# Two moves around the seam between an attention and a quantized feed-forward: where a small chain of scale arithmetic runs, and in which order the LoRA factors are written

## The reference, cut to what matters

```python
x = x + tanh(g_xattn[0]) * L0_xattn(layernorm(x), ctx, ctx)      # linear attention
x = x + tanh(g_ffn[0])   * L0_ffn(layernorm(x), ...)             # NF4 weights with LoRA, width 2752
x = x + tanh(g_xattn[1]) * L1_xattn(layernorm(x), ctx, ctx)      # autocorrelation attention by FFT
x = x + tanh(g_ffn[1])   * L1_ffn(layernorm(x), ...)             # linear layer with LoRA and column norm

def L0_ffn(x1, ...):
    Wg, Wu, Wd = (NF4[codes] * absmax per 64, transposed)        # three dequantized matrices
    y1 = x1 @ Wg + x1 @ g_lora_a @ g_lora_b
    y2 = x1 @ Wu + x1 @ u_lora_a @ u_lora_b
    x3 = relu(y1) * y2
    return x3 @ Wd + x3 @ d_lora_a @ d_lora_b
```

## Time and profile before

| what | value |
|---|---|
| median of 3 executions | 2161.8 us (2161.77 to 2164.0) |
| profiled execution | 2167.11 us, its span 2165.1 us |
| TensorE busy | 2052.2 us, 95% of the span, mean granted clock 0.977 |
| VectorE, ScalarE, GpSimd busy | 51%, 54%, 31% |
| attention | about 0 to 180.5 us |
| feed-forward | about 180.8 to 1600 us |
| tail | to 2165.1 us |

### The profile page before, as it was taken

How to read it: one execution, slowest core, us unless ns; L and a number is a source line. 1 busy time by engine, 2 the same in 40 slices (tenths; PEclk the granted TensorE clock), 3 DMA queues, 4 the chain that set the end, 5 groups by cost and what they waited for, 6 DMA issues and landing times. The chain is left out here.

```text
span 2165.1 us, 25964 instructions
## 1 busy us (share of the span) xinstructions
PE 2052.2 (95%) x9634; PEld 1023.6 (47%) x9634; DVE 1098.7 (51%) x1951; ACT 1175.9 (54%) x1851; POOL 663.7 (31%) x640
## 2 busy tenths in 40 slices
PE   7985999999999999999999999999975899999997
PEld 5772444444444444444444444444432455555543
DVE  5774252442624335253352524335257788888852
ACT  6993755656566565665656566565613334344321
POOL 3432211112121121211112121121225676667741
PEclk9997999999999999999999999999987899999999
DMA  6632211112122121221221111111130011111000
GB/s 222 201 127 61 77 49 59 48 51 70 58 65 69 55 69 54 69 69 55 64 63 55 49 55 49 55 49 51 44 125 24 12 40 49 49 49 46 13 30 29
DMA packets 64925, 136.76 MB, mean 63 GB/s; under 512 B 8992, under 2 KB 13728, under 8 KB 64800
## 3 DMA queue, kind: packets, MB, share of 16 engines
q1 hardware_dynamic: 64800, 135.11, 19.1%
HBM read 122.49 MB, written 12.58 MB: 62 GB/s over the span
## 5 line engine op out<-in xcount | busy, mean ns | idle before, releaser
L682 ACT ACTIVATE first<-first 128x512 f32<-128x512 int32 x1008 | 632.7, 628 | 28.0
L920 PE MATMUL ps_ring<-xT_hi,gu_hi 128*128 128x512 f16 x1376 | 524.2, 381 | 1.7 <-POOL gu_lo L758 1.7
L920 PE MATMUL ps_ring<-xT_lo,gu_hi 128*128 128x512 f16 x1376 | 523.7, 381 | 0.0
L920 PE MATMUL ps_ring<-xT_hi,gu_lo 128*128 128x512 f16 x1376 | 523.2, 380 | 0.0
L812 DVE SCALAR_TENSOR_TENSOR wt<-first,w_scale,absm 128x512 f32<-128x512 f32 x132 | 98.8, 749 | 478.5 <-ACT first L682 477.4
L758 POOL TENSOR_TENSOR gu_lo<-wt,gu_hi 128x512 f16<-128x512 f32 x88 | 102.6, 1166 | 765.2 <-ACT gu_hi L688 765.2
L831 DVE SCALAR_TENSOR_TENSOR X<-ps_ring,ffn_gain,X 128x512 f32<-128x512 f32 x352 | 259.8, 749 | 135.3 <-PE ps_ring L943 135.3
L943 PE MATMUL ps_ring<-dn_hi,hid_hi 128*128 128x512 f16 x704 | 266.9, 379 | 0.0
L943 PE MATMUL ps_ring<-dn_hi,hid_lo 128*128 128x512 f16 x704 | 266.7, 379 | 0.0
L943 PE MATMUL ps_ring<-dn_lo,hid_hi 128*128 128x512 f16 x672 | 254.6, 379 | 0.0
L920 PEld LDWEIGHTS ps_ring<-xT_hi,gu_hi 128*128 128x128 f16 x1376 | 135.1, 98 | 171.7 <-issue 14.5
(11 more groups left out here) (203 smaller groups left out, 2683.1 us busy)
## 6 DMA issues: line engine op xcount, KB each, us to landing
first<-in_codes SPq DMA_DIRECT2D x132, 256.0 KB, 2.8
absm<-in_absmax SPq DMA_DIRECT2D x264, 128.0 KB, 3.0
X<-in_x SPq DMA_DIRECT2D x16, 512.0 KB, 4.3
c_in<-in_ctx SPq DMA_DIRECT2D x16, 512.0 KB, 5.3
cT<-in_ctxT SPq DMA_DIRECT2D x16, 512.0 KB, 3.6
xT_hi<-in_ctx SPq DMA_DIRECT2D x8, 1024.0 KB, 7.1
out<-X SPq DMA_DIRECT2D x16, 512.0 KB, 2.6
wide<-in_w SPq DMA_DIRECT2D x8, 512.0 KB, 4.7
```

Source lines behind the costliest of these rows:

```text
L682: act.activation(level[u % 2][:], codes[u % RING] if k == 0 else level[u % 2][:], ACT.Prelu, bias=bias, scale=scale, alpha=alpha).then_inc ...
L920: mm = pe.matmul(o[:], w[c][:, m, k, :], xx[:, k, ts], start=(q == 0), stop=(q == 3 * KD - 1))
```

## The change

Two edits. First, the scales' parts now run inside middle steps. With AT = 9: SyncE issues the three bound loads before the loads of b = 4; ScalarE squares at the start of step 8; VectorE reduces in step 9, reads the maxima in step 10, the spread results in step 11 and runs the chain of tiny results in step 13, each time right after `kvm` and ahead of the offset of line 465; TensorE's three small products stand in steps 10 and 11, after the product of line 434, in an upper part of `psE`, and two waits are added ahead of the turning of `ek` in steps 11 and 12 (`left`); GpSimd's square roots stand at the start of step 12. One more small copy is made (`every[:, 9:12]` is read apart). Second, at the opening of the feed-forward the LoRA factors are written in the order of use: `lora_b` first, then m = 0 and the first unit, m = 1 and the second unit, and m = 2 and `l_gain` after all six units. TensorE waits for each m only before the first unit that uses it.

```diff
-    ps_top, ps_all = ps[0:9, 0:P], ps[:, BANK:BANK + 12]
+    ps_top, ps_all = ps[0:9, BANK:BANK + P], ps[:, BANK + 2 * P:BANK + 2 * P + 12]
+    AT = 9
-    OWN, DIAG, EVERY = 6, 8, 9
+    OWN, READ, DIAG, EVERY = 6, 8, 9, 10
     def pool_part(pool, i):
-        if i == TILES:
+        if i == AT + 3:
     def act_part(act, i):
-        if i == TILES - 2:
+        if i == AT - 1:
     def pe_part(pe, i):
-        if i == TILES:
+        if i == AT + 1:
             pe.wait_ge(step, OWN)
-            pe.matmul(ps_top, own[:, 0:9], ident[:], start=True, stop=True).then_inc(top_mm, 1)
             pe.wait_ge(const_set, 3)
             pe.matmul(ps_all[:, 9:12], ones[:], own[:, 9:12], start=True, stop=True)
+            pe.matmul(ps_top, own[:, 0:9], ident[:], start=True, stop=True).then_inc(top_mm, 1)
+        if i == AT + 2:
             pe.wait_ge(step, DIAG)
             pe.matmul(ps_all[:, 0:9], ones[0:9, :], diag[:], start=True, stop=True).then_inc(all_mm, 1)
     def dve_part(dve, i):
-        if i == TILES - 1:
+        if i == AT:
             dve.wait_ge(squared, 3)
...
-        if i == TILES:
+        if i == AT + 1:
             dve.wait_ge(top_mm, 1)
             dve.reduce_max(top[:], ps_top, AX.X).then_inc(step, 1)
-            dve.wait_ge(step, 7)
+            dve.tensor_copy(every[:, 9:12], ps_all[:, 9:12]).then_inc(step, 1)
+            dve.wait_ge(step, 8)
             dve.tensor_scalar(diag[:], ident[0:9, 0:9], top[:], None, ALU.mult).then_inc(step, 1)
+        if i == AT + 2:
             dve.wait_ge(all_mm, 1)
-            dve.tensor_copy(every[:], ps_all).then_inc(step, 1)
-        if i == TILES + 1:
+            dve.tensor_copy(every[:, 0:9], ps_all[:, 0:9]).then_inc(step, 1)
+        if i == AT + 4:
             dve.wait_ge(norms_done, 1)
...
+    def left(pe, i):
+        if i == AT + 2:
+            pe.wait_ge(step, READ)
+        if i == AT + 3:
+            pe.wait_ge(step, EVERY)
...
+                    if b == 4:
+                        scales_sp(sp)
...
-                scales_sp(sp)
```

```diff
 ScalarE, opening of the feed-forward
                 act.wait_ge(la_in, 48)
-                for m in range(3):
+                lora_parts(0)
+                for m in range(2):
                     act.activation(lora_a[:, m], la_f[m], ACT.Copy, scale=ab_scale[0:LROWS, 0:1]).then_inc(la_hi, 1)
-                lora_parts(0)
                 for u in range(AHEAD):
                     w_hi(0, u)
+                    if u == 3:
+                        act.activation(lora_a[:, 2], la_f[2], ACT.Copy, scale=ab_scale[0:LROWS, 0:1]).then_inc(la_hi, 1)
 VectorE
-                for m in range(3):
+                def lora_wide(m):
                     dve.wait_ge(la_hi, m + 1)
                     dve.scalar_tensor_tensor(lora_a[32:64, m], ...).then_inc(la_done, 1)
                 lora_parts(0)
+                lora_wide(0)
+                weights(0, 0, first=True)
+                lora_wide(1)
+                weights(0, 1, first=True)
+                for u in range(2, AHEAD):
+                    weights(0, u)
+                lora_wide(2)
                 dve.wait_ge(mag_in, 16)
                 dve.tensor_scalar(l_gain[:], ...).then_inc(gain_done, 1)
-                for u in range(AHEAD):
-                    weights(0, u, first=u < 2)
 TensorE
+                    if j == 0 and u in (0, 2, 8):
+                        pe.wait_ge(la_done, m + 1)
...
-                pe.wait_ge(la_done, 3)
```

More of the change, by code:

```diff
@@ L192, in dve_part @@
             dve.reduce_max(ab[:], norms[:, 3:9].rearrange("p (s m) -> p s m", s=2), AX.X).then_inc(step, 1)
-            dve.wait_ge(step, 12)
+            dve.wait_ge(step, 13)
             dve.scalar_tensor_tensor(own[:, 0:3], max_q, TINY, M[:], ALU.max, ALU.add).then_inc(step, 1)
@@ L196, in dve_part @@
             dve.tensor_scalar(ab[:], ab[:], TINY, None, ALU.max).then_inc(step, 1)
-            dve.wait_ge(step, 15)
+            dve.wait_ge(step, 16)
             dve.tensor_tensor(N[:], ratio[:], N[:], ALU.add).then_inc(step, 1)
@@ L201, in dve_part @@
             dve.tensor_copy(M[:, 2:3], own[:, 2:3]).then_inc(step, 1)
-            dve.wait_ge(step, 18)
+            dve.wait_ge(step, 19)
             dve.reciprocal(rM[:], M[:]).then_inc(step, 1)
@@ L205, in dve_part @@
             dve.tensor_tensor(abp[:], ab[:, 0:1], ab[:, 1:2], ALU.mult).then_inc(step, 1)
-            dve.wait_ge(step, 21)
+            dve.wait_ge(step, 22)
             dve.reciprocal(rN[:], N[:]).then_inc(step, 1)
@@ L210, in dve_part @@
             dve.tensor_scalar(res["ab_scale"][:], rab[:], ABMAX, None, ALU.mult).then_inc(step, 1)
-            dve.wait_ge(step, 25)
+            dve.wait_ge(step, 26)
             dve.tensor_scalar(res["lora_gain"][:], res["w_scale"][:], abp[:], ABMAX ** -2, ALU.mult, ALU.mult).then_inc(step, 1)
@@ L215, in dve_part @@
             dve.scalar_tensor_tensor(nn[:], M[:, 2:3], D / (WMAX * HMAX), nn[:], ALU.mult, ALU.mult).then_inc(step, 1)
-            dve.wait_ge(step, 28)
+            dve.wait_ge(step, 29)
             dve.scalar_tensor_tensor(res["hid_gain"][:], ratio[:, 0:1], HMAX / (D * WMAX ** 2 * LN_SCALE ** 2), ratio[:, 1:2], ALU.mult, ALU.mult).then_inc(step, 1)
@@ L220, in dve_part @@
             dve.tensor_tensor(res["ffn_gain"][:], nn[:], tg[:, 2:3], ALU.mult).then_inc(step, 1)
-            dve.wait_ge(step, 30)
-    return sp_part, pool_part, act_part, pe_part, dve_part
+            dve.wait_ge(step, 31)
+    def left(pe, i):
[3 more added lines that the diff above has]
+            pe.wait_ge(step, EVERY)
+    return sp_part, pool_part, act_part, pe_part, dve_part, left
 def exists(i):
@@ L275, in phase_linear_attention, with run @@
         const_in, gates_in, const_set, tanh_done = (sem(n) for n in ("const_in", "gates_in", "const_set", "tanh_done"))
-        scales_sp, scales_pool, scales_act, scales_pe, scales_dve = ffn_scales(nc, ctx, io, res, psB, const_set, tanh_done)
-        def run(engine, step, scales):
-            for i in range(4):
+        scales_sp, scales_pool, scales_act, scales_pe, scales_dve, scales_left = ffn_scales(nc, ctx, io, res, psE, const_set, tanh_done)
+        def run(engine, step):
+            for i in range(TILES + 3):
                 step(i, i % 2)
[L282 to L287, removed]
         with nc.Block() as block:
@@ L334, in step @@
                 def step(i, h):
+                    scales_pool(pool, i)
                     if exists(i - 1):
@@ L348, in _ @@
                     rsqrt(h, h, mv, ve, rstd, mv_done, ve_done, rstd_done)
-                run(pool, step, scales_pool)
+                run(pool, step)
             @block.scalar
@@ L375, in step @@
                 def step(i, h):
+                    scales_act(act, i)
                     if exists(i):
@@ L405, in _ @@
                 act.activation(tg[:], gates[:], ACT.Tanh).then_inc(tanh_done, 1)
-                run(act, step, scales_act)
+                run(act, step)
             @block.tensor
@@ L435, in step @@
                         mm.then_inc(kv_mm, 1)
+                        scales_pe(pe, i)
                         pe.wait_ge(rSx_done, i + 1)
@@ L448, in _ @@
                 pe.wait_ge(const_in, 32)
-                run(pe, step, scales_pe)
+                run(pe, step)
             @block.vector
@@ L507, in _ @@
                 dve.wait_ge(tanh_done, 1)
-                run(dve, step, scales_dve)
+                run(dve, step)
 def phase_nf4_ffn(nc, io, res):
```

2 lines of the change are left out of this document (added).

## The result

The changed kernel takes 2167.46 us (median of 9, 2166.1 to 2169.2), the kernel before 2161.41 (9 runs beside it). The ratio is 1.0028, with a 95% interval of 1.0018 to 1.0039: 6.1 us slower, between 3.9 and 8.4.

The account below looks back on a forecast made before the run. TensorE is busy from about 192 us, so the first large feed-forward product's start decides. Middle steps 4.6 us later, last steps 1.5 and opening 1.1 gained: +2.0 on 2161.8 gives 2163.8 us, range 2160 to 2168.5.

Parts of the forecast that it names:

- rival A: Middle steps: TensorE loses its clock after idling in two places, 4.8 us more, median 2168.6; chance 0.15.
- The view of what bounds the kernel: TensorE is busy from about 192 us, so the first large feed-forward product's start moves the end by as much.
- Squares: ScalarE's squares at the start of step 8: 2.36 us less 0.53 idle, cost 1.83 us, bounds 1.3 to 2.4.
- Reductions: VectorE's reductions in step 9 ahead of nmr: cost 1.8 us, bounds 1.0 to 2.8.
- Small steps, loads, waits of `left`, square roots: Steps 10 to 12 and the earlier bound loads: each fits idle time and costs nothing, at most 0.3 us for some.
- Chain: VectorE's tiny results in step 13 ahead of nmr: 2.37 us long, cost about 0.95 us, bounds 0.4 to 1.9.
- Last steps: End of the attention: without the squares, eq of step 15 begins earlier, 1.5 us gained, bounds 1.0 to 2.4.
- Opening: Start of the feed-forward: reordered LoRA factors bring the large product earlier, 1.1 us gained, bounds 0 to 1.6.
- Sum: Whole kernel: 4.6 - 1.5 - 1.1 = +2.0 us, median 2163.8.
- B: Middle steps hide more than granted: cost 2.8 us, median 2162.0, or 2160.5 with gains at upper bounds; chance 0.12.
- C: First large product's half-clock ramp, worth 2.9 us, falls away or lasts longer (up to +1); chance 0.06 for several us gained.
- D: Start of the feed-forward: the loads land late, gain 0, median 2164.9; chance 0.07.

Follow-up runs that it names:

- before_again: The kernel before with no edit, profiled a second time; ratio 1.0004 to before, span 2158.6 us.
- chain_columns: Changed kernel with the chain from p_nn on as one-column, one-tensor instructions (six more) and tile 12's nmr in that form; ratio 1.0002 to before.
- chain_pointer: Changed kernel with the chain from p_nn on and both nmr offsets using one tensor and a factor read from SBUF; ratio 1.0017 to before.
- chain_first: Changed kernel with one chain instruction, p_nn, taking its second factor as a scalar operand; one run, step 13 to 14 took 12.23 us.
- only_scales: Kernel before with only the scales moved into middle steps, the feed-forward's opening left as before; ratio 1.0036 to before.
- spread_squares: Kernel before with squares in seven pieces over steps 7 to 13, one-tensor nmr in all steps, second unit ahead of m = 1; ratio 0.9980 to before.
- the run called opening: Changed kernel with the second unit's weights ahead of the low part of m = 1; ratio 1.0019 to before.

## Why the prediction was right and where it was not

The side (slower) and the range held; the size was a third of the measured one, and the outcome was one that I had given 0.19. That the time lies in the range is in part luck: the prediction took the upper end, 2168.5, from rival A, whose cost did not come, and what brought the time near it was one term outside its own bounds.

- *The view of what bounds the kernel.* Right as far as the runs can tell, with one exception. The loss is made in the steps and carried through: the feed-forward column is the same within its scatter. Nine edited kernels have a ratio. In eight of them it agrees, within its interval, with how much later or earlier than in before_again the large product starts behind step 0. In chain_columns it does not (4.5 us later, ratio at most 2.4), and that stays open.
- *Squares, 1.83 us.* Measured 1.72 (11.04 against 9.32).
- *Reductions, 1.8 us.* Measured 1.97. The missing 0.2 is again a meeting with `eq`: `nmr` behind them took 0.51 instead of 0.16 us. In chain_pointer, where `nmr` has one tensor, the same step is only 1.62 us longer than its neighbours (10.99 against 9.37).
- *Small steps, loads, waits of `left`, square roots: nothing.* Measured nothing: the distances of steps 8 to 9 and 10 to 13 are 9.31 to 9.33.
- *Chain, 0.95 us, bounds 0.4 to 1.9.* Measured 2.97, outside its own bounds. This is the mis-sized term. I took the chain's 2.37 us from a place where GpSimd was idle and laid it into a step where `eq` begins 1.25 us after `kvm` ends (146.43 and 145.18). The chain's own length was priced well: chain_columns, which has no wait, loses 1.65 us with six more instructions, and without the 0.6 us that I estimated for these it would be 1.05. The other 1.9 us are the wait, which the sum did not have. chain_first shows that the wait belongs to no single instruction, chain_columns that it goes when no wide or two-tensor instruction is left. A row that would have warned me stood in the trace of before and I did not look for it: VectorE's timeline of step 1 had a `nmr` of 2.30 us beside `eq`.

```profile
30.07 2.30 DVE L465 SCALAR_TENSOR_TENSOR nmr<-mv,rstd 128x1 f32<-128x1 f32 x1 [0.84 <-POOL rstd L332]
```

- *Last steps, 1.5 us gained.* Measured 1.0 against before_again, 1.6 against the first profile. The two differ because TensorE's product into `psO` of step 16, which stands behind 2.7 to 3.0 us of idling, ran partly at half clock, and not for the same time: it took 2.76 us in before_again, 3.38 in before and 3.19 in the changed kernel, where 1.98 is full speed. The mechanism came as said: `eq` of step 15 starts 12.86 us after the row of step 14 instead of 14.38, 1.5 earlier. That put it beside `nmr` of tile 14, a meeting that the kernel before did not have and my sum neither. In chain_pointer that `nmr` does not wait, and the column is hardly shorter (31.19 for 31.33).

```profile
167.28 2.34 POOL L343 TENSOR_TENSOR eq<-rSx,eq 128x1024 f32<-128x1024 f32 x1
167.34 2.29 DVE L472 SCALAR_TENSOR_TENSOR nmr<-mv,rstd 128x1 f32<-128x1 f32 x1 [0.84 <-POOL rstd L335]
```

- *Opening, 1.1 us gained.* Measured 0.3. The load's landing was right to 0.1 us; the missing 0.8 is the second scaling beside GpSimd (1.53 for 0.75). Two smaller errors cancel: m = 1 cost 1.4 us where I had 1.2, and unit 1's low part took 1.15 instead of 1.51. My 5.37 us from the first unit to the product held only for the old order, in which that scaling ran before GpSimd began.
- *Sum.* With the measured terms 6.7 - 1.0 - 0.3 = 5.4, and the runs say 6.1 (3.9 to 8.4).
- *Rivals.* A: TensorE's clock did fall once in a middle step. In step 14 it idled 2.20 us ahead of line 440, whose product then took 3.62 us, with a granted clock of 0.50 from 154 to 156 us:

```profile
153.03 3.62 PE L440 MATMUL psE<-cT,ekT 128*128 128x128 f32 x16 [2.20 <-ACT ekT L384]
```

  At 0.93 us (step 8) and 1.20 us (step 10) of idling the same product took 2.05 us. The length of the idling alone does not decide it: in only_scales the same product follows the same 2.20 us (at 152.30) and takes 2.05 us. These two are also the test of the cost: step 14 to 15 takes 8.62 us in both, so the fall cost nothing. B is refuted: nothing was absorbed. C: by the granted clock, TensorE stays at its lower level for 4.1 us from the start of the large product in the changed kernel, 4.9 in before_again and 6.0 in before. That is worth a few tenths between the first two. In only_scales it was 2.7 us, so this scatters by itself. D nearly gave its number (0.3 us gained instead of 0), but not by its mechanism: the load landed when I had said.

The cost of switching tables that I had weighed did not come: ScalarE's squares stand between copies without a gap, in the changed kernel (88.75 to 91.10) as in spread_squares. The rule that bore on the case was another. The Trainium skill, "SBUF — State Buffer", section SBUF: two separate sides, says that VectorE and GpSimd share a pair of ports which the one that starts first holds for its whole instruction, and that a VectorE instruction takes part if it has two inputs in SBUF or runs in a mode that uses both ports. The runs here fit it: 2.0 us for two tensors and for three or four columns, 0.14 to 0.20 us for one tensor of one column. No trace shows in which mode an instruction ran, so why the width decides for one tensor is not shown.

## What to carry to other kernels

Price a moved instruction by what runs beside it at its new place, not by its row at the old one: a result of 128 numbers took 2.2 us longer because GpSimd was multiplying. Work laid into a loop without slack is free only in pieces no longer than the idle time of the engine that takes it (0.48 us into 0.53), and what runs in the shadow of a pipeline's end needs no move at all. A profile can stand 5 us off its kernel's median, so small changes are read from distances between rows around the edit, not from spans.

## What the runs showed of the hardware

- VectorE beside a GpSimd multiplication of 2.36 us: `tensor_tensor` 128 x 1 2.05 us, `tensor_scalar` 128 x 3 and 128 x 4 2.06 us with either kind of factor, `tensor_scalar` 128 x 1 0.14 us (factor in the instruction) or 0.20 us (factor from SBUF). bn_stats and the maximum were not held up (1.29 and 1.17 us with `eq` beside them and without).
- It works the other way too: GpSimd's low part took 1.58 us instead of 1.16 where VectorE's m = 1 was running when it began (191.93), and 1.80 instead of 1.51 in the run called opening.
- The tail after the feed-forward took 555.1 to 560.7 us in twelve profiled executions of the same code. In the longest, chain_columns, the granted clock was 0.98 from 2000 to 2100 us where before_again had 1.00. What decides that I did not test.
